# Moving three weight jobs in the attention stage: SyncE's requests, GpSimd's products and ScalarE's conversions at other places of their queues

## The reference

```python
    xn = _layernorm(x, axis=-1)                       # x: 2 x 1024 x 512
    # attention, 32 heads of 16, q and k layer-normed over all 512, ALiBi, causal
    scores = jnp.einsum('bqhd,bkhd->bhqk', q, k) * scale + slopes * rel
    probs = jax.nn.softmax(jnp.where(causal, scores, -1e30), axis=-1)
    s = jnp.einsum('bhqk,bkhd->bqhd', probs, v) @ Wout.T
    # MLP: weights are integers, dequantized by rows of 128
    w = (imatrix - repeat(zeros, 128)) * repeat(scales, 128)
    g = _silu((jax.nn.silu(xn @ gate) * (xn @ up)) @ down)
    return x + s * g
```

## Time and profile before

| | |
|---|---|
| median of 3 runs | 1349.84 us (1346.81 to 1351.06) |
| profiled execution, its time | 1358.14 us |
| profiled execution, its span | 1356.1 us |
| PE busy | 1213.4 us (89%) |
| DVE busy | 741.4 us (55%) |
| ACT busy | 617.3 us (46%) |
| POOL busy | 501.5 us (37%) |
| mean granted TensorE clock | 0.940 |

### The profile page before, as it was taken

The page is one execution under the profiler, slowest core; times in us unless marked ns, Lnnn a source line. Parts: engine busy times, 40 slices in busy tenths (PEclk is TensorE's granted clock), DMA queues, the critical chain, the costliest instruction groups (busy, mean ns, idle before and its releaser), DMA issues. The chain is left out here.

```text
span 1356.1 us, 22935 instructions
## 1 busy us (share of the span) xinstructions
PE 1213.4 (89%) x7168; PEld 801.3 (59%) x7168; DVE 741.4 (55%) x1153; ACT 617.3 (46%) x923; POOL 501.5 (37%) x512
## 2 busy tenths in 40 slices
PE   6899986889888888888888876999999999999997
PEld 5677743434433434444434324888888878888886
DVE  6778895656666666566666514235433542453223
ACT  3333313556565555556566563433343343333332
POOL 2756630212121121112121122455455545545553
PEclk9999976889899889888899877999999999999999
DMA  6343554654566354756655332010210021002000
GB/s 214 95 141 94 158 147 111 152 119 121 152 104 144 94 115 108 159 110 136 125 112 137 96 109 84 11 54 0 89 37 33 1 94 52 12 18 75 0 1 31
DMA packets 112248, 123.63 MB, mean 91 GB/s; under 512 B 29648, under 2 KB 83408, under 8 KB 112080
## 3 DMA queue, kind: packets, MB, share of 16 engines
q1 hardware_dynamic: 85744, 110.14, 31.6%
q10 hardware_dynamic: 26464, 12.98, 3.5%
HBM read 92.80 MB, written 29.88 MB: 90 GB/s over the span
## 5 line engine op out<-in xcount | busy, mean ns | idle before, releaser
L266 DVE TENSOR_REDUCE mx<-bank 128x1 f32<-128x512 f32 (+3 forms) x608 | 371.1, 658 | 213.1 <-PE bank L278 212.1
L922 ACT ACTIVATE pr<-pair 128x1024 f32<-128x1024 f32 (+3 forms) x384 | 297.0, 810 | 267.0 <-PE pair L1012 237.2
L1136 POOL TENSOR_TENSOR ws_lo<-w_f,ws_hi 128x512 fp32r<-128x512 f32 x168 | 247.0, 1497 | 262.2 <-ACT ws_hi L1177 262.2
L1296 DVE TENSOR_TENSOR sg<-pair,sg 128x512 f32<-128x512 f32 x56 | 38.7, 692 | 260.0 <-ACT sg L1224 260.0
L1359 PE MATMUL pair<-xc_hi,ws_lo 128*128 128x512 f32 x448 | 175.2, 391 | 1.4 <-DVE xc_lo L1279 1.4
L1359 PE MATMUL pair<-xc_lo,ws_hi 128*128 128x512 f32 x448 | 175.0, 391 | 0.0
L1359 PE MATMUL pair<-xc_hi,ws_hi 128*128 128x512 f32 x448 | 174.8, 390 | 0.0
L1224 ACT ACTIVATE sg<-pair 128x512 f32<-128x512 f32 x56 | 33.5, 598 | 235.7 <-PE pair L1359 235.7
L276 PE MATMUL bank<-identb,behind 128*128 128x512 bf16 x128 | 60.4, 472 | 69.9 <-DMA ks<-in_krows 39.2
L895 POOL TENSOR_TENSOR w_f<-w_f,zst 128x896 f32 (+1 forms) x24 | 50.1, 2087 | 195.1 <-ACT zst L937 195.1
L278 PE MATMUL bank<-xin_c,s_sb 108*128 108x128 bf16 (+3 forms) x576 | 115.7, 307 | 5.4 <-DVE mx L266 4.9
(11 more groups left out here) (95 smaller groups left out, 1936.3 us busy)
## 6 DMA issues: line engine op xcount, KB each, us to landing
stk<-parts ACTq DMA_DIRECT2D x16, 768.0 KB, 5.7
zst<-in_z_all SPq DMA_DIRECT2D x24, 448.0 KB, 4.3
sst<-in_s_all SPq DMA_DIRECT2D x24, 448.0 KB, 5.1
w_f<-in_w_all SPq DMA_DIRECT2D x24, 448.0 KB, 7.1
oscr<-ot SPq DMA_DIRECT2D x32, 256.0 KB, 2.5
xin_c<-in_x SPq DMA_DIRECT2D x32, 256.0 KB, 2.7
s_sb<-stk SPq DMA_DIRECT2D x96, 64.0 KB
xin_c<-stk SPq DMA_DIRECT2D x96, 64.0 KB
```

The source lines that it names most:

```text
L266: dve.tensor_reduce(dst, b[:, 0:n_heads * w].rearrange("p (j c) -> p j c", c=w), AX.X, ALU.max).then_inc(m_free, 1)
L922: act.activation(pr[e % NPR][:, 2 * p:2 * p + 2, 0:w], pair[p][:, :, 0:w], ACT.Exp, scale=SCALE)\
L1136: return pool.tensor_tensor(dst, src, hi.bitcast(F32), ALU.subtract)
L1296: dve.tensor_tensor(sg[s][:, :], pair[s][:, 1, :], sg[s][:, :], ALU.mult).then_inc(h_mul, 1)
```

## The change

Three things move, on three engines. SyncE asks for job 3ip + 3 behind the first half of the load of the next keys and queries instead of ahead of it, in odd groups. GpSimd computes the first job of even groups between the two chains instead of after both. ScalarE converts ahead of steps 1 and 10 in even groups (before: ahead of step 6 and after the last copy), and ahead of step 5 in odd groups (before: 6).

```diff
-        JOB_AT = 6
+        JOBS_AT = ((1, 10), (5,))
...
                     store_o(i, 0)
-                    if not last:
-                        half_job(3 * ip + (1, 3)[s])
+                    if s == 0:
+                        half_job(3 * ip + 1)
                     if last is None:
 
                         sp.wait_ge(s_full[1], full(i, LOW_KEYS - 1))
                         apart(sp, "sp")
                         load(sp, i + 2, s, 0)
+                    if s == 1 and not last:
+                        half_job(3 * ip + 3)
+                    if last is None:
 
                         sp.wait_ge(s_full[1], full(i, NSTEP - 1))
                         apart(sp, "sp")
...
                     chain(pool, dneg1, 2 * i + 1)
+                    if s == 0:
+                        job(3 * ip)
                     if not last:
 
                         pool.wait_ge(neg0_done, i + 2)
                         pool.wait_ge(m_full, base(i) + at("D1", last) + TURNS)
                         chain(pool, dneg0, 2 * i + 2)
-                    job(3 * ip + (0, 2)[s])
-                    if s == 0:
-                        job(3 * ip + 1)
+                    job(3 * ip + 1 + s)
...
-                        if e == JOB_AT:
-                            convert(3 * ip + (0, 2)[s])
+                        if e in JOBS_AT[s]:
+                            convert(3 * ip + (2 if s else JOBS_AT[s].index(e)))
...
                     copy_o(i, 1)
-                    if s == 0:
-                        convert(3 * ip + 1)
```

## The result

The changed kernel took 1360.76 us (median of 6 runs, 1356.24 to 1364.40), the kernel before in the same comparison 1348.32 us (6 runs, 1337.81 to 1351.06). The ratio is 1.0102 (95% interval 1.0062 to 1.0143): slower by 1%. In a second comparison of 6 and 17 runs it is 1.0127 (1.0085 to 1.0169). The runs of the kernel before spread widely, from 1334.6 to 1354.3 us over all comparisons; the profiled execution shown ahead of the prediction, 1358.14 us, lies above all of them.

A forecast was written before the change was run, and what follows sets the result against it. TensorE's 65.9 us of waits for loads were taken to bound the kernel and to become waits for weights. Turns -2.7, first group +12.3, last group -6.5 gave +3.1 us: span 1359, median 1353 us, range 1330 to 1371.

The forecast's parts named there:

- The load's first half: Load of next keys and queries, at group starts: TensorE's wait 0, at most 1.2 us; alone worth 100 us.
- Odd groups: Conversion ahead of step 5: ScalarE waits 5 us for weights, slow clock 2.0; turn 20.4 us against 19.0.
- Even groups: Conversion ahead of step 1: TensorE's step 2 3.05 us late, slow clock 2.0; step 10 adds 0.4; turn 17.3 us.
- First group: ScalarE waits for job 0's weights; TensorE's step 2 moves 10.3 us, slow clock 2.0: 12.3 us more, once.
- Last group: First copy comes 4.9 us earlier and the 1.6 us conversion behind it goes: 6.5 us less.
- The prediction's sign of it: Last group, new profile: TensorE's wait for d1, the row maxima, 5 us less than the 3.01 us group's before.
- 14 turns: Stretches from a group's second copy to the next group's first: 263.9 us against 266.6, 2.7 us less.
- the surviving gain: Rival, 0.20: weights land in 5.7 us or the clock stays up in the moved waits; time 1323 to 1328 us.
- the dearer waits: Rival, 0.17: ScalarE's weights land at 9.1 us, 2.0 more per odd and 1.2 per even turn; time 1375 us.
- The late second half: Rival, 0.05: load's second half, behind the weights, costs 1 to 3 us on some even turns; 1357 to 1370 us.
- the rule weighed: One engine's descriptors go in ring order, so the load's second half cannot pass the weights; 3.1 us, hidden by the stall.

The follow-up runs named there:

- the kernels with a late odd conversion: Kernels converting ahead of step 7 instead of 5 in odd groups; the changed kernel with this alone: 1301.38 us, ratio 0.9694 to the kernel before.
- second profiles: Kernel before and changed kernel each run once more, unchanged: 1347.38 us (1 run) and 1361.03 us, the latter at ratio 1.0127.
- the kernel with both late: Changed kernel with conversions ahead of steps 3 and 10 in even groups and 7 in odd ones: 1279.04 us, ratio 0.9544 to the kernel before.

## Why the prediction was right, and where it was off

**The load's first half.** Right: the waits for it are gone but for one of 1.66 us in the turn into group 1, and the free turn is 11.87 us in the kernels with a late odd conversion. The prediction had worked out 11.85 from two slow turns.

**Odd groups.** Right in both terms. The weights were asked at 503.81 in the pair shown, 9.8 us after the copy (9.7), and landed 16.7 us after it (16.8); the turn was 18.6 (18.4) and the slow clock cost the rest 1.87 us (2.0). A slow stretch followed the wait in all 14 turns of the changed kernel, the shortest of them 2.00 us; that a wait longer than 2.29 us always brings one is not so (see the last section).

**Even groups.** Right in mechanism, 0.2 us too dear: weights asked 1.4 us before the copy instead of 1.9 and landed at 5.4 instead of 6.0; turn 17.06 instead of 17.3. The second conversion, ahead of step 10, cost nothing instead of 0.4 (rest 18.93).

**First group.** 12.3 us predicted. The first copy moved by 13.2 us between the first two profiles, of which 2.0 were there already at TensorE's start (222.23 against 220.22): 11.2.

**Last group.** The mechanism of the turn was right, the rest was mis-sized. Predicted 6.5 us less; turn and rest together went from 36.4 to 32.9 us, 3.5 less. The turn gave 4.6 of the 4.9 expected. ScalarE sent d1 8.7 us after the copy at 783.83 in the kernel before and 3.8 us after the one at 793.41 in the changed one (ScalarE's timelines, in this order):

```profile
792.49 0.73 ACTq L324 DMA_DIRECT2D qs<-dt  x1
...
797.21 0.75 ACTq L324 DMA_DIRECT2D qs<-dt  x1
```

The prediction's sign of it, 5 us less wait for d1, did not come: the wait grew from 3.01 to 4.37 us. Counted from the copy, d1 landed 5.5 us sooner, but TensorE was ready for it 6.9 us sooner. The rest grew by 1.0 instead of losing 1.6. The last conversion stood behind the first copy in the kernel before, at 806.34; now it stands ahead of it, at 807.07, where it holds up the exponentials. TensorE waited for ScalarE again, and a second slow stretch followed (timelines of the changed kernel, then its windows):

```profile
804.60 1.04 PE L1008 MATMUL pair<-qs,ks 111*128 111x512 bf16 x4 [4.37 <-DMA qs<-dt]
...
810.32 0.60 PE L1008 MATMUL pair<-qs,ks 111*128 111x512 bf16 x2 [1.44 <-ACT pr L925]
...
807.07 0.95 ACT L939 ACTIVATE w_f<-w_f 128x896 f32<-128x896 int32 x1
...
812.00:814.00 2.00, 2.00 (x16) 0.31 (x8) 0.00 (x0) 1.00 (x2) 1.40 (x1) 0.58 0.30 108
814.00:816.00 2.00, 2.00 (x11) 0.43 (x4) 0.00 (x0) 0.12 (x1) 0.00 (x0) 0.57 0.26 97
```

The kernel before has a slow stretch behind its wait for d1 too, but stays at 1.00 from 806 to 822.

**The base.** The sum said 3 us more where the medians are 12 apart. The differences of the profiles, in us, with each group's rest counted in:

| part | predicted | first profiles | second profiles |
|---|---|---|---|
| up to the first copy | +12.3 | +13.2 | +10.7 |
| 14 turns | -2.7 | -3.7 | +5.7 |
| last group | -6.5 | -3.5 | -2.1 |
| after the last copy | 0 | -2.4 | -2.5 |
| sum | +3.1 | +3.6 | +11.8 |

The largest error is the 14 turns. The turns of the kernel before were counted as 266.6 us from one long execution, and the result was then added to a median 8 us lower. An ordinary execution of it has turns of 255.7 us, and the prediction's 263.9 for the turns after the change (measured 262.9 with the longer rest counted in, 261.4 in the second profile) is then 8 us more and not 2.7 less. The last group was priced too high as well, and the part behind the last copy, taken as unchanged, became 2.4 us shorter; I did not look for its cause. That the sum agrees with the first pair of profiles to 0.5 us is partly luck: the last group's 3.0 us too little and these 2.4 cancel. The time lies inside the range because the range was wide enough for the base.

The 14 turns of the kernel before took 266.6 and 255.7 us in its two profiles, and single ones from 15.7 to 21.0. Those of the changed kernel agree within 2 us in the sum (262.9 and 261.4), though single even turns still vary from 14.3 to 19.5. That the kernel before varies because its load races with the weights is my reading of it; no run isolates it. Whatever is late by chance in the profiled execution should be scaled to the median before a steady cost is set against it.

**The rivals.** Neither the surviving gain nor the dearer waits came: landings were 6.8 and 6.9 us in the pair shown, 5.6 to 7.8 over all 24 with a median of 6.4, and the clock did fall. The late second half exists, hidden. On the rule weighed, the prediction took the landing 6.0 us after the last request as agreement; but those weights landed at about 514.95 (507.05 and 7.9), ahead of krows' request at 515.05. So neither trace tests whether a load can pass the weights.

What was not tried: asking for the zeros and integers apart, and a place for the third job at which neither half of a load stands behind it.

## What to carry to other kernels

A wait taken from one engine's queue is worth what the next latest arrival leaves: before moving work forward, set the landing of its data beside the place where the engine will ask for it. With one buffer between request, conversion and use, every place shifts all later ones in the ring, and two moves that each gain 1% can lose 1% together; move the consumer to where the data are, then the request. A stall of TensorE costs twice where it brings the slow clock, here some 2 us on top.

## What the runs showed of the hardware

I had not expected that the slow clock would need so little, nor that the length of a wait would not decide it. In the changed kernel a wait of 2.42 us brought 0.50 for about 3 us. In the kernel with both late, a wait of 1.71 us (at 365.94, shown above) did not, one of 1.80 us did, and one of 3.24 us, longer than either, did not (TensorE's timeline, then windows of that kernel behind the three waits):

```profile
623.02 0.50 PE L276 MATMUL bank<-identb,behind 128*128 128x512 bf16 x1 [1.80 <-DMA ks<-in_krows]
...
689.62 0.39 PE L276 MATMUL bank<-identb,behind 128*128 128x512 bf16 x1 [3.24 <-DMA ks<-in_krows]
...
364.00:366.00 2.00, 0.29 (x6) 0.12 (x4) 1.19 (x4) 0.65 (x2) 1.87 (x1) 1.00 1.28 206
366.00:368.00 2.00, 2.00 (x15) 0.90 (x19) 1.41 (x3) 0.97 (x2) 1.81 (x2) 1.00 0.17 64
...
624.00:626.00 2.00, 2.00 (x6) 0.61 (x4) 1.37 (x2) 1.02 (x1) 1.81 (x3) 0.50 0.00 0
...
690.00:692.00 2.00, 2.00 (x23) 0.90 (x23) 1.73 (x3) 1.30 (x2) 1.82 (x3) 1.00 0.05 12
```

So the same kind of wait may or may not cost the extra 2 us, and these runs do not show what decides it. In the odd turns of the changed kernel, with waits of about 6 us, it came every time.

Nor had I expected how much the same program varies in the turns in which it waits for a load: fourteen turns summed to 266.6 us in one execution and 255.7 in another, at the same 18.93 us between the copies.
